# Mixer of a three-part decoder layer: output weight and residual addition on VectorE, behind the multiplication by the inverse deviation, in place of GpSimd

## Chip, cores and metric

The kernel runs on one core of one Trainium2 chip. The time is the device time of one execution in microseconds. PE is TensorE, DVE is VectorE, ACT is ScalarE, POOL is GpSimd and SP is SyncE.

## What is computed

Eight sequences of 256 tokens with 256 features go through three parts, each with a residual addition. The change lies in the second part, the mixer (an mLSTM cell with 4 heads of 64 features), which works on each batch by itself:

```python
x = x + attn(layernorm(x), ...)            # state-space block and gated MLP
x = x + xattn(layernorm(x), ctx, ctx, ...) # the mixer, below
x = x + ffn(layernorm(x), ...)             # FP4-rounded gate, up and down matrices

# mixer, per batch and head
D = exp(log_D - max_log_D)
C = (q @ k.T / sqrt(64)) * D
h = (C / normaliser) @ v
h_norm = (h - mean(h)) / sqrt(var(h) + 1e-5)
h_norm = h_norm * (1.0 + out_w)            # output weight, one number per feature
# transposed back to tokens x features and added to x
```

## The kernel before

The program is written out engine by engine. Semaphores named after events (`hn_ready`, `x2_ready` and so on) tie the engines together, and each engine takes its own instructions strictly in the written order. A batch is two tiles of 128 tokens. `x_res` holds all of x in SBUF as 128 x 16 x 256.

The work has two phases. `front` is the state-space block with its MLP. After it comes `mixer_and_ffn`, in which the mixer (8 batches) and the last part (16 tiles of 128 tokens) run as software pipelines. In each step of a pipeline an engine calls its list of stages, each with a lag: in step s a stage with lag 3 works on batch s - 3. `pipelines` writes the first steps of the mixer out, runs steps 3 to 6 as a hardware loop of two steps in a pass, and then writes out steps in which mixer stages and last-part stages stand in one list (from step 7, five steps). Then comes a loop of the last part alone.

On DVE a mixer step has these stages: `weights` for both chunks (L1541, three multiplications of scores by weights, reading PSUM), `variance` (L1575, sum of squares), `normalise` (the small instructions L1553 to L1560 on the denominators, L1564 twice, the mean L1568, the subtraction L1570) and `scale` (L1580, the multiplication by the inverse deviation `rv`):

```python
mixer = [(lambda b, p: weights(b, p, 0), 1), (lambda b, p: weights(b, p, 1), 1), (variance, 3),
         (normalise, 2), (scale, 3)]
```

ACT computes the exponentials (L1483) and the squares (L1490). POOL has `rstds` (L1635 and L1637, which make `rv` from the sum of squares by a power) and `residual` (L1642, the output weight; L1645, the addition to `x_res`). `normalise` begins with a wait for the additions of earlier batches, because it overwrites the buffer of `h` (two buffers, named `scores` in the profile since they lie in that region) that the addition read:

```python
dve.wait_ge(s["x2_ready"], LEAD + C * (b - 1))
```

In the last part, per tile, DVE takes statistics (L1586, L1591), POOL makes deviation and shift (`tile_rstd`, L1654 to L1660), ACT normalises (L1525), and DVE rounds the tile with the `Quantiser` (L318 to L336; `xq` is its copy for the input, 256 wide, `hq` the one for the hidden rows, 704 wide). PE turns the tile (L1432), multiplies by gate and up (L1443), turns the hidden rows (L1453) and multiplies by down (L1462). DVE adds the result to x (L1618), and SP stores it.

Of the kernel before, what the change touches and what calls it, by code (L numbers as in the profile page):

```python
# [23 lines left out]
ALU = mybir.AluOpType  # L24
# [5 lines left out]
C = S // P  # L30
# [19 lines left out]
LEAD = 8  # L50
# [21 lines left out]
def inner(ap, n):  # L72

    return ap.unsqueeze(len(ap.shape)).to_broadcast([*ap.shape, n])


def middle(ap, n):

    return ap.unsqueeze(1).to_broadcast([ap.shape[0], n, ap.shape[1]])


def carry(eng, m):


    eng.sem_inc(m.carried, 1)
# [51 lines left out]
def pipelines(eng, units, stages, next_units, next_stages, begin, overlap):  # L137


    depth = depth_of(stages) if stages else 0  # L140
    if stages:
        for s in range(depth):
            step(units, stages, s)
        steady(eng, units, stages, depth, min(units, begin))
        for s in range(min(units, begin), begin):
            step(units, stages, s)
    for s in range(overlap):
        step(units, stages, begin + s)
        step(next_units, next_stages, s)
    steady(eng, next_units, next_stages, overlap, next_units)  # L150
    for s in range(next_units, next_units + overlap):
        step(next_units, next_stages, s)
# [1122 lines left out]
def mixer_and_ffn(m):  # L1275
# [14 lines left out]
    h = over_s("h", [P, 2, C * XH, XD])  # L1290
# [4 lines left out]
    s = m.counts["mlstm"]  # L1295
# [29 lines left out]
    @block.sync  # L1325
    def _(sp):
        def load_r(b, p):
            sp.wait_ge(m.max_stored, 16)
            sp.wait_ge(s["arg1_ps"], LEAD + b - 1)
            carry(sp, m)  # L1330
            sp.dma_start(rmax[0:3, p, :].rearrange("j (h t) -> j h t", h=XH),
                         m.rows_dram[bass.ds(b * XH, XH), :, :].rearrange("h j t -> j h t")).then_inc(r_in[p], 16)

        def load_qk(b, p):
            sp.wait_ge(s["qk_ps"], LEAD + C * (b - 1))
            carry(sp, m)
            sp.dma_start(kT[:, p, :, :], m.a["ctxT"][:, :, bass.ds(b * S, S)]).then_inc(arrived[p], 16)
            sp.dma_start(qT[:, p, :, :].rearrange("p k t -> p (k t)"), row(m.xnT, b)).then_inc(arrived[p], 16)

        def load_v(b, p):  # L1340
            sp.wait_ge(s["num_ps"], LEAD + b - 1)
            carry(sp, m)
            for c in range(C):
                sp.dma_start(v[:, p, c, :].rearrange("p (h e) -> p h e", h=XH)[:, :, 0:XD],
                             m.a["ctx"][bass.ds((C * b + c) * P, P), :].rearrange("p (h e) -> p h e", h=XH))\
                  .then_inc(v_in[p], 16)

        sp.wait_ge(t["ones_set"], 1)
        for b in range(2):
            load_qk(b, b)  # L1350
            load_v(b, b)
        for b in range(2):
            load_r(b, b)

        pipeline(sp, B - 2, [(lambda b, p: load_r(b + 2, p), 0), (lambda b, p: load_qk(b + 2, p), 0),
                             (lambda b, p: load_v(b + 2, p), 0)])


        def store(t, p):
            sp.wait_ge(f["y_ready"], LEAD + t + 1)  # L1360
            sp.dma_start(m.out[bass.ds(t, 1), :, :].rearrange("o p d -> (o p) d"), y[:, p, :])\
              .then_inc(y_out[p], 16)

        pipeline(sp, T, [(store, 0)])
        for each in y_out:
            sp.wait_ge(each, LEAD + 16 * (T // 2))
# [166 lines left out]
    def _(dve):  # L1533
        def weights(b, p, c):
            n = C * b + c
            w, done = ((w0, s["w0_exp"]), (w1, s["w1_exp"]))[c]
            dve.wait_ge(s["qk_ps"], LEAD + n + 1)
            dve.wait_ge(done, LEAD + b + 1)
            for k in range(2 if c == 0 else 1):
                mine = (w[:, p, 2 * k:2 * k + 2, :] if c == 0 else w[:, p, :, :]).rearrange("p k t -> p (k t)")  # L1540
                last = dve.scalar_tensor_tensor(mine, bank[3 + k if c == 0 else 5][:], XD ** -0.5, mine, ALU.mult,  # L1541
                                                ALU.mult)
            last.then_inc(s["w_ready"], 1)
# [33 lines left out]
        def scale(b, p):  # L1577
            dve.wait_ge(s["v_rstd"], LEAD + b + 1)
            hp = h[:, p, :, :]
            dve.tensor_tensor(hp, hp, inner(rv[:, p, :], XD), ALU.mult).then_inc(s["hn_ready"], 1)  # L1580


        def tile_stats(t, p):
# [31 lines left out]
        def output(t, p):  # L1615
# [7 lines left out]

        mixer = [(lambda b, p: weights(b, p, 0), 1), (lambda b, p: weights(b, p, 1), 1), (variance, 3),
                 (normalise, 2), (scale, 3)]
        forward = [(product, 3), *first, (tile_stats, 0), (output, 5), (tile_mean, 0), *last]
        pipelines(dve, B, mixer, T, forward, BEGIN, OVERLAP)

    @block.gpsimd
    def _(pool):  # L1630
        def rstds(b, p):
            pool.wait_ge(s["v_ready"], LEAD + b + 1)
            pool.wait_ge(s["hn_ready"], LEAD + b - 1)
            carry(pool, m)
            pool.tensor_scalar(var[:, p, :], var[:, p, :], 1.0 / XD, LN_EPS, ALU.mult, ALU.add).then_inc(s["v_mean"], 1)  # L1635
            pool.wait_ge(s["v_mean"], LEAD + b + 1)
            pool.tensor_tensor(rv[:, p, :], var[:, p, :], m.minus_half[:, 0:C * XH], ALU.pow).then_inc(s["v_rstd"], 1)  # L1637

        def residual(b, p):
            pool.wait_ge(s["hn_ready"], LEAD + b + 1)  # L1640
            rows = h[:, p, :, :].rearrange("p (c h) e -> p c (h e)", c=C)
            pool.tensor_tensor(rows, rows, middle(m.out_w[:], C), ALU.mult).then_inc(s["hn_scaled"], 1)  # L1642
            pool.wait_ge(s["hn_scaled"], LEAD + b + 1)
            here = m.x_res[:, bass.ds(C * b, C), :]
            pool.tensor_tensor(here, here, rows, ALU.add).then_inc(s["x2_ready"], C)  # L1645

        pool.memset(rmax[:], 0.0)
        pool.memset(v[:], 1.0).then_inc(t["ones_set"], 1)


        def tile_rstd(t, p):
            pool.wait_ge(f["f_mv_ready"], LEAD + t + 1)
            carry(pool, m)
            pool.tensor_scalar(ve[:, p, :], mv[:, p, 1:2], LN_EPS, None, ALU.add).then_inc(f["f_ve_ready"], 1)  # L1654
            pool.wait_ge(f["f_ve_ready"], LEAD + t + 1)
            pool.tensor_tensor(rstd[:, p, :], ve[:, p, :], m.minus_half[:, 0:1], ALU.pow).then_inc(f["f_rstd_ready"], 1)
            pool.wait_ge(f["f_rstd_ready"], LEAD + t + 1)
            pool.wait_ge(f["xf_norm"], LEAD + t - 1)
            carry(pool, m)
            pool.tensor_scalar(shift[:, p, :], mv[:, p, 0:1], rstd[:, p, :], -1.0, ALU.mult, ALU.mult)\  # L1660
                .then_inc(f["f_shift_ready"], 1)

        mixer = [(rstds, 3), (residual, 3)]
        forward = [(tile_rstd, 0)]
        pipelines(pool, B, mixer, T, forward, BEGIN, OVERLAP)

# [50 lines left out]
```

## Time and profile before

| | |
|---|---|
| time, median of 3 runs | 661.98 us (651.65, 661.98, 662.48) |
| the profiled execution's own time | 652.93 us |
| its span in the trace | 651.2 us |
| busy: PE, DVE, ACT, POOL | 590.7, 464.6, 242.1, 161.1 us |
| mean granted TensorE clock | 0.953 of full speed |

The span is the time from the first to the last instruction in the trace. Busy times are sums over the whole span; what an engine is worth in one stretch has to be read there. A mean over a group of instructions can hide a few long ones.

### The profile page before, as it was taken

How to read it: one execution, taken by the hardware profiler on the slowest of the kernel's cores; microseconds unless marked ns; L12 is line 12 of the kernel's file. 1: busy time of each engine (PE TensorE's matmuls, PEld its weight loads, DVE VectorE, ACT ScalarE, POOL GpSimd, SP SyncE). 2: the span in 40 equal slices, each digit the busy share in tenths (PEclk: the TensorE clock that was granted, in tenths of full speed). 3: DMA queues.
4: the chain of work that ended last, by engine and by line, in shares of the span. 5: the costliest groups of instructions: out<-in, count | busy, mean ns of one | idle time of the engine just before them, and what ended most of it. 6: DMA issues, size and time to landing. Idle time of an engine off the chain costs nothing. (4 is left out here: it accounts for less than half of the span.)

```text
span 651.2 us, 9629 instructions
## 1 busy us (share of the span) xinstructions
PE 590.7 (91%) x3055; PEld 470.7 (72%) x3055; DVE 464.6 (71%) x983; ACT 242.1 (37%) x532; POOL 161.1 (25%) x199
## 2 busy tenths in 40 slices
PE   5997898699999889899999999869976699999996
PEld 5766465478888778778888888858864466666664
DVE  4999599868886233443444456457898999999994
ACT  1643665744555421211111110154532344444432
POOL 3163003125454101111011010202766322222200
PEclk8997999879999999999999999699985899999999
DMA  9100000000000230000000000134410000000000
GB/s 317 59 1 1 0 2 15 7 5 6 6 4 2 83 147 0 1 1 0 17 17 17 2 17 16 30 90 117 127 49 2 0 10 16 16 16 16 16 17 24
DMA packets 22527, 20.99 MB, mean 32 GB/s; under 512 B 12120, under 2 KB 20696, under 8 KB 22104
## 3 DMA queue, kind: packets, MB, share of 16 engines
q1 hardware_dynamic: 21720, 19.22, 9.2%
q10 hardware_dynamic: 768, 1.26, 0.6%
q8 instruction: 22, 0.36, 0.2%
q14 instruction: 17, 0.14, 0.1%
HBM read 16.04 MB, written 2.34 MB: 28 GB/s over the span
## 5 line engine op out<-in xcount | busy, mean ns | idle before, releaser
L722 PE MATMUL ps<-xnT,w_fc 128*128 128x256 f32 x512 | 112.6, 380 | 0.0
L722 PEld LDWEIGHTS ps<-xnT,w_fc 128*128 128x128 f32 x512 | 96.5, 190 | 12.7
L1443 PE MATMUL ps<-w_fc,scores 128*128 128x352 f32 x256 | 82.9, 478 | 5.9 <-ACT scores L1512 5.9
L1076 DVE TENSOR_TENSOR xs<-ps,xs 128x512 f32<-128x512 f32 x32 | 22.1, 692 | 72.9 <-ACT xs L903 72.9
L1443 PEld LDWEIGHTS ps<-w_fc,scores 128*128 128x128 f32 x256 | 49.1, 197 | 33.3 <-ACT scores L1512 7.4
L903 ACT ACTIVATE xs<-ps 128x512 f32<-128x512 f32 x32 | 19.1, 597 | 107.5 <-PE ps L722 69.9
L735 PE MATMUL ps<-zs,xs 128*128 128x256 f32 x256 | 56.6, 379 | 0.0
L735 PEld LDWEIGHTS ps<-zs,xs 128*128 128x128 f32 x256 | 48.6, 190 | 6.6
L974 DVE SCALAR_TENSOR_TENSOR fold<-xpad,conv_w,fold 128x256 f32<-128x256 f32 x120 | 51.4, 483 | 0.9
L1462 PE MATMUL ps<-u_res,hT 128*128 128x256 f32 x192 | 47.3, 388 | 2.7 <-DVE scores L1618 1.7
L1462 PEld LDWEIGHTS ps<-u_res,hT 128*128 128x128 f32 x192 | 34.9, 189 | 14.8 <-issue 5.3
L624 PE MATMUL ps<-xnT,fold 128*128 128x256 f32 x160 | 39.8, 400 | 2.4 <-ACT xpad L825 2.4
L624 PEld LDWEIGHTS ps<-xnT,fold 128*128 128x128 f32 x160 | 30.2, 199 | 9.8 <-ACT xpad L825 5.8
L561 POOL TENSOR_SCALAR q_ve<-q_mv 128x2 f32<-128x2 f32 x8 | 1.8, 222 | 142.1 <-DVE q_mv L1092 142.1
L543 POOL TENSOR_TENSOR bc<-xs,head_c 128x512 f32<-128x512 f32 x16 | 24.5, 1536 | 49.5 <-DVE zs L1060 29.8
L674 PE MATMUL ps<-xpad,fold 128*128 128x64 f32 x256 | 32.8, 284 | 0.0
L969 DVE TENSOR_SCALAR fold<-xpad,conv_w 128x256 f32<-128x256 f32 x40 | 26.1, 683 | 8.2 <-ACT xpad L825 8.2
L674 PEld LDWEIGHTS ps<-xpad,fold 128*128 128x128 f32 x256 | 31.6, 201 | 0.1
L632 PE MATMUL ps<-fold,xnT 128*128 128x512 f32 x64 | 30.9, 627 | 0.0
L697 PE MATMUL ps<-w_out,xF 128*128 128x256 f32 x128 | 30.2, 380 | 0.3 <-DVE u_res L1067 0.3
L697 PEld LDWEIGHTS ps<-w_out,xF 128*128 128x128 f32 x128 | 23.7, 190 | 6.4 <-issue 3.8
L1483 ACT ACTIVATE xs<-ps,a_tok 128x256 f32<-128x256 f32 (+1 forms) x64 | 20.8, 437 | 18.1 <-PE ps L1379 18.1
(256 smaller groups left out, 1159.0 us busy)
## 6 DMA issues: line engine op xcount, KB each, us to landing
xs<-in_ctxT SPq DMA_DIRECT2D x16, 256.0 KB, 3.3
zs<-in_ffn_w SPq DMA_DIRECT2D x1, 2112.0 KB, 9.4
x_res<-in_x SPq DMA_DIRECT2D x8, 256.0 KB, 7.5
w_fc<-in_w_fc SPq DMA_DIRECT2D x1, 2048.0 KB, 10.4
xs<-xnT SPq DMA_DIRECT2D x8, 256.0 KB, 3.4
xs<-in_ctx SPq DMA_DIRECT2D x16, 128.0 KB, 2.6
out<-scores SPq DMA_DIRECT2D x16, 128.0 KB, 1.7
fold<-in_w_in ACTq DMA_DIRECT2D x2, 580.0 KB, 5.4
```

Of the source, the lines that this page charges most:

```text
L543: pool.tensor_tensor(heads(dx[:, c, :]), heads(m.xs[:, n, :]), inner(m.head_c[:, 2, :], HD), ALU.mult)\
L624: last = pe.matmul(bank[1 + n % 2][:, 0:S], w_in[:, kk, w0:w0 + P], turned_u(b, kk), start=(kk == 0), stop=(kk == KD - 1))
L632: last = pe.matmul(bank[3 + c][:], turned_u(b, kk)[:, c * P:(c + 1) * P], w_in[:, kk, 0:DI], start=(kk == 0), stop=(kk == KD - 1))
L674: last = pe.matmul(bank[2 + c][:, h * HD:(h + 1) * HD], E[:, p, c, h * P:(h + 1) * P], dtx[:, p, c, h * HD:(h + 1) * HD], start=True, stop ...
L697: last = pe.matmul(bank[6][:, c * D:(c + 1) * D], ygT[:, c, k * P:(k + 1) * P], m.w_out[:, k, :], start=(k == 0), stop=(k == DI // P - 1))
L722: last = pe.matmul(bank[half + r][:, i * S:(i + 1) * S], m.w_fc1[:, kk, col:col + P], m.xnT[:, b, kk * S:(kk + 1) * S], start=(kk == 0), s ...
L735: last = pe.matmul(bank[4 + c][:, 0:D], hid[:, p, k, c * P:(c + 1) * P], w_fc2[:, k, :], start=(k == 0), stop=(k == KM - 1))
L969: dve.tensor_scalar(conv[:, p, k, :], xpad[:, p, k, 0:S], m.conv_w[:, ch, 0:1], None, ALU.mult).then_inc(s["conv_step"], 1)
L974: dve.scalar_tensor_tensor(conv[:, p, k, :], xpad[:, p, k, tap:tap + S], m.conv_w[:, ch, tap:tap + 1], conv[:, p, k, :], ALU.mult, ALU.add)\
L1076: dve.tensor_tensor(hid[:, p, 2 * pair:2 * pair + 2, :].rearrange("p k t -> p (k t)"), bank[r][:], gate[:, r, :], ALU.mult).then_inc(g["hi ...
L1443: last = pe.matmul(bank[1 + j][:, 0:HALF], xT[:, p, k * P:(k + 1) * P], m.w_gu[:, k, j * HALF:(j + 1) * HALF], start=(k == 0), stop=(k == ...
L1462: last = pe.matmul(bank[7][:, 0:D], hT[0:w, p, k, :], m.w_dn[0:w, k, :], start=(k == 0), stop=(k == KF - 1))
```

## The change

Of each batch, the two instructions of `residual` move from POOL to DVE and are written right behind `scale`. The semaphores and the values waited for are the same ones. POOL's list of mixer stages keeps `rstds` alone. In the changed kernel the two instructions are L1583 and L1586, and the lines behind them move by 6 on DVE.

```diff
@@ -1578,6 +1578,12 @@
             dve.wait_ge(s["v_rstd"], LEAD + b + 1)
             hp = h[:, p, :, :]
             dve.tensor_tensor(hp, hp, inner(rv[:, p, :], XD), ALU.mult).then_inc(s["hn_ready"], 1)
+            dve.wait_ge(s["hn_ready"], LEAD + b + 1)
+            rows = hp.rearrange("p (c h) e -> p c (h e)", c=C)
+            dve.tensor_tensor(rows, rows, middle(m.out_w[:], C), ALU.mult).then_inc(s["hn_scaled"], 1)
+            dve.wait_ge(s["hn_scaled"], LEAD + b + 1)
+            here = m.x_res[:, bass.ds(C * b, C), :]
+            dve.tensor_tensor(here, here, rows, ALU.add).then_inc(s["x2_ready"], C)
@@ -1635,14 +1641,6 @@
-        def residual(b, p):
-            pool.wait_ge(s["hn_ready"], LEAD + b + 1)
-            rows = h[:, p, :, :].rearrange("p (c h) e -> p c (h e)", c=C)
-            pool.tensor_tensor(rows, rows, middle(m.out_w[:], C), ALU.mult).then_inc(s["hn_scaled"], 1)
-            pool.wait_ge(s["hn_scaled"], LEAD + b + 1)
-            here = m.x_res[:, bass.ds(C * b, C), :]
-            pool.tensor_tensor(here, here, rows, ALU.add).then_inc(s["x2_ready"], C)
@@ -1660,7 +1658,7 @@
-        mixer = [(rstds, 3), (residual, 3)]
+        mixer = [(rstds, 3)]
```

On DVE, at the end of the second step in a pass of the mixer loop, the rows change as follows (`scores` is the buffer of `h`, `rv` the inverse deviation):

```order
@@ -516,4 +519,7 @@
 L1570 SCALAR_TENSOR_TENSOR scores<-h_mean,scores 128x512 [waits post]
 L1580 TENSOR_TENSOR scores<-scores,rv 128x512 [waits v_rstd]
+L1583 TENSOR_TENSOR scores<-scores,out_w 128x512 [waits hn_ready]
+L1586 ISA [waits hn_scaled]
+L1586 TENSOR_TENSOR x_res<-x_res,scores 128x512
 L118 REGISTER_ALU
 L118 COMPARE_AND_BRANCH
```

Two instructions stand behind the scale now, and the second has its wait in an instruction of its own.

On DVE, where mixer and last part stand in one list, the scale of a batch was followed by the quantiser of a tile:

```order
@@ -546,4 +554,6 @@
 L1570 SCALAR_TENSOR_TENSOR scores<-h_mean,scores 128x512 [waits post]
 L1580 TENSOR_TENSOR scores<-scores,rv 128x512 [waits v_rstd]
+L1583 TENSOR_TENSOR scores<-scores,out_w 128x512 [waits hn_ready]
+L1586 TENSOR_TENSOR x_res<-x_res,scores 128x512 [waits hn_scaled]
 L318 TENSOR_REDUCE xq_amax<-scores 128x16 [waits xq_step,xf_norm]
 L320 TENSOR_SCALAR xq_scale<-xq_amax 128x16 [waits xq_step]
```

The two instructions now stand ahead of the quantiser on the same engine.

On POOL, the same place of the program, before:

```order
L1635 TENSOR_SCALAR var<-var 128x8 [waits v_ready,hn_ready]
L1637 TENSOR_TENSOR rv<-var,minus_half 128x8 [waits v_mean]
L1642 TENSOR_TENSOR scores<-scores,out_w 128x512 [waits hn_ready]
L1645 TENSOR_TENSOR x_res<-x_res,scores 128x512 [waits hn_scaled]
L1654 TENSOR_SCALAR f_ve<-f_mv 128x1 [waits f_mv_ready]
L1656 TENSOR_TENSOR f_rstd<-f_ve,minus_half 128x1 [waits f_ve_ready]
```

and in the changed kernel:

```order
L1641 TENSOR_SCALAR var<-var 128x8 [waits v_ready,hn_ready]
L1643 TENSOR_TENSOR rv<-var,minus_half 128x8 [waits v_mean]
L1652 TENSOR_SCALAR f_ve<-f_mv 128x1 [waits f_mv_ready]
L1654 TENSOR_TENSOR f_rstd<-f_ve,minus_half 128x1 [waits f_ve_ready]
L1658 TENSOR_SCALAR f_shift<-f_mv,f_rstd 128x1 [waits f_rstd_ready,xf_norm]
```

Nothing of POOL's queue stands between the inverse deviation of a batch and the small instructions of a tile any more.

## Rows read from the trace of the kernel before

**Rows 1.** Waits, 420 to 515 us: waiter, releaser, total us, times, longest.
```profile
DVE den L1553 <- POOL x_res L1645: 2.0, 4, 0.6
DVE scores L1580 <- POOL rv L1637: 2.4, 1, 2.4
```

**Rows 2.** Chain of waits, one batch of the mixer loop: start us, us, what.
```profile
460.09 0.69 DVE scores L1580
460.85 1.29 POOL scores L1642
462.36 1.27 POOL x_res L1645
```

**Rows 3.** Timeline of DVE, one step of the mixer loop.
```profile
460.69 1.88 DVE L1541 SCALAR_TENSOR_TENSOR xs<-ps,xs 128x512 f32<-128x512 f32 x3
462.49 0.68 DVE L1575 TENSOR_REDUCE var<-scores 128x8 f32<-128x512 f32 x1
463.65 0.17 DVE L1553 TENSOR_SCALAR den<-ps 128x8 f32<-128x8 f32 x1 [0.49 <-POOL x_res L1645]
...
465.40 0.69 DVE L1568 TENSOR_REDUCE h_mean<-scores 128x8 f32<-128x512 f32 x1
466.12 0.69 DVE L1570 SCALAR_TENSOR_TENSOR scores<-h_mean,scores 128x512 f32<-128x512 f32 x1
466.73 0.69 DVE L1580 TENSOR_TENSOR scores<-scores,rv 128x512 f32<-128x512 f32 x1
467.33 1.88 DVE L1541 SCALAR_TENSOR_TENSOR xs<-ps,xs 128x512 f32<-128x512 f32 x3
```

**Rows 4.** Windows of one loop step and of the slow-clock stretch: busy by engine, clock.
```profile
core 0: us, PE busy (x) PEld busy (x) DVE busy (x) ACT busy (x) POOL busy (x), PEclk, DMA share, GB/s
...
466.70:473.30 6.60, 5.79 (x47) 4.98 (x47) 5.81 (x14) 3.23 (x9) 4.38 (x4) 1.00 0.56 153
...
486.80:496.20 9.40, 4.56 (x21) 3.97 (x20) 8.84 (x20) 1.64 (x3) 5.58 (x7) 0.50 0.01 3
```

**Rows 5.** Chain of waits where PE takes over, and one gate group later.
```profile
515.10 1.50 PE ps L1453 x6
516.60 5.80 PE ps L1443 x16
...
526.20 4.90 PE ps L1443 x16
```

**Rows 6.** Instructions of line L1558, register part: times in ns, min/median/max.
```profile
L1558 DVEq FUSED_REGOPS  x4: 57/64/64, 450.8 to 470.7; - x4
```

**Rows 7.** Timeline of DVE in the written-out steps.
```profile
483.04 0.68 DVE L1575 TENSOR_REDUCE var<-scores 128x8 f32<-128x512 f32 x1
483.63 0.16 DVE L1553 TENSOR_SCALAR den<-ps 128x8 f32<-128x8 f32 x1
...
485.97 0.69 DVE L1570 SCALAR_TENSOR_TENSOR scores<-h_mean,scores 128x512 f32<-128x512 f32 x1
486.79 0.69 DVE L1580 TENSOR_TENSOR scores<-scores,rv 128x512 f32<-128x512 f32 x1
```

**Rows 8.** Timeline of DVE and POOL beside the quantiser.
```profile
487.56 1.26 POOL L1642 TENSOR_TENSOR scores<-scores,out_w 128x512 f32<-128x512 f32 x1 [0.80 <-DVE scores L1580]
487.85 1.01 DVE L320 TENSOR_SCALAR xq_scale<-xq_amax 128x16 f32<-128x16 f32 x1
...
488.98 1.26 POOL L1645 TENSOR_TENSOR x_res<-x_res,scores 128x512 f32<-128x512 f32 x1
489.18 1.34 DVE L324 SCALAR_TENSOR_TENSOR xq_v<-xq_inv,scores 128x256 f32<-128x256 f32 x1
...
507.69 0.96 DVE L320 TENSOR_SCALAR xq_scale<-xq_amax 128x16 f32<-128x16 f32 x1
...
509.13 0.36 DVE L324 SCALAR_TENSOR_TENSOR xq_v<-xq_inv,scores 128x256 f32<-128x256 f32 x1
```

**Rows 9.** Lines L320 and L324, input quantiser: ns min/median/max, first and last start.
```profile
L320 DVE TENSOR_SCALAR xq_scale<-xq_amax x16: 156/165/1008, 487.9 to 620.4; 128x16 f32<-128x16 f32 x16
L324 DVE SCALAR_TENSOR_TENSOR xq_v<-xq_inv,scores x16: 360/361/1341, 489.2 to 621.1; 128x256 f32<-128x256 f32 x16
```

## Prediction

> **The bound.** I read first where the two moved operations lie in the program, then who waits for whom there, then the order of DVE's own instructions, because the work moves onto DVE. The span is 651.2 us and the profiled execution took 652.93, so 1.73 us lie outside it. The moved operations run only between 453.5 and 508.6 us. In the view of waits for the mixer [rows 1] DVE waits four times, 2.0 us in all, for POOL's residual addition, and once, 2.4 us, for POOL's inverse deviation. The chain of waits [rows 2] confirms the first one: scale on DVE (460.09), output weight on POOL (460.85), addition on POOL (462.36), and 3.56 us after the scale began, DVE's `normalise` of a later batch (463.65). A reader of the chain alone would say that POOL bounds this loop.
>
> The timeline of DVE says something else [rows 3]. One step of the loop is 6.64 us, from the L1541 group at 460.69 to that at 467.33. DVE works through all of it except the 0.49 us ahead of L1553. The POOL part of the chain lies beside work that DVE has to do anyway: three multiplications of weights (L1541, 1.80 us until the next start) and the variance sum (L1575). So DVE's own queue and the loop through POOL are nearly equal, and DVE is the one that has almost nothing left to give. PE is busy 5.79 of 6.60 us in a step at full clock [rows 4], but it waits for nobody's output on the chain there. After 515.10 us the chain is PE's all the way to 634 us (each tile has one gate and up group, as at 526.20, [rows 5]). A delay of DVE before 515.10 is therefore passed on whole to the end, and nothing after it hides or enlarges it.
>
> **Added work.** The output weight and the addition do not run on DVE in this trace, but `scale` itself (L1580, 0.69 us) is a TENSOR_TENSOR of the same size and type with both inputs in SBUF. I take its duration. What counts on the queue is the distance between starts. Where the next instruction needs the result of the one before, it is 0.72 us: L1568 at 465.40, L1570 at 466.12 [rows 3]. Where it does not, it is 0.60: L1580 at 466.73, L1541 at 467.33. Before, `scale` took 0.60 of the queue. After, scale to weight is 0.72, weight to addition 0.72, addition to the next group 0.60, together 2.04. The cost is 2.04 - 0.60 = 1.44 us per batch, and for 8 batches 11.5 us. The bounds are 8 x 1.20 = 9.6 (no dependent gap) and 8 x 1.6 = 12.8 (a further 0.16 each). In the loop, which runs for the first four batches, the addition gets its place in `x_res` from a register, and the order shows a separate instruction for the wait in front of it. The nearest thing is L1558, which takes its place from a register too: four times, once for each pass through a loop step, DVE's sequencer spends 0.06 us on it [rows 6]. With the separate wait I take 0.1 us x 4 = 0.4, with bounds 0 and 0.5.
>
> **Removed time.** (1) The wait at L1553 for the addition. By starts, L1575 to L1553 is 463.65 - 462.49 = 1.16 us in the loop, and 0.59 where nothing waits (483.04 to 483.63, [rows 7]). The difference is 0.57; the four places have 0.56, 0.57, 0.56 and 0.66, together 2.35 us (the 2.0 of [rows 1] is without the overlap of starts). After the change the addition is earlier in DVE's own queue, so this wait is gone entirely. Next late there would be PE's sums, but PE works 5.8 us per step [rows 4] against DVE's new 7.6. Or scale would wait for POOL's inverse deviation: POOL's two small instructions are 4.38 - 1.28 - 1.27 = 1.83 us [rows 2, 4], behind the 0.68 of L1575 and with some 0.4 for the handing over, so 2.9 us after L1575 begins; DVE asks 466.73 - 462.49 - 0.57 = 3.67 after it. That is late by nothing. (2) A short wait of scale for POOL's inverse deviation for batch 5, where POOL came late because of its two long instructions: 0.82 us from L1570 at 485.97 to L1580 at 486.79 [rows 7] in place of 0.61 (466.12 to 466.73), so 0.2 us. The later wait of 2.4 us [rows 1] stays: POOL runs the tile's three small instructions ahead of batch 7's deviation, and both start from DVE results whose distance does not change. DVE keeps its idle 2.4 us there, in front of the added work and not behind it, so it hides none of it.
>
> (3) The largest and least visible term. In three places the quantiser's small instructions take far longer than elsewhere [rows 8]: L320 1.01 us at 487.85 and 0.96 at 507.69, L324 1.34 us at 489.18, though their medians over 16 are 0.165 and 0.361 [rows 9]. Each time they end with an instruction of POOL: POOL's output weight runs from 487.56 to 488.82 and L320 ends at 488.86; POOL's addition runs from 488.98 to 490.24 and L324 ends at 490.52, that is 0.28 us later. At 509.13 POOL is idle, and the same L324 takes 0.36. The next batch repeats the pattern (L320 1.01, L324 1.34). So while POOL runs one of its two long two-input instructions, these DVE instructions stand still. With the change POOL has none left. The gain is 2 x (0.84 + 0.98) + 0.79 = 4.4 us, bounds 0 and 4.4. The DVE instructions beside POOL in the loop (L1541, which reads PSUM, and the one-input L1575) have their usual 0.68 us each, so nothing is to be gained there.
>
> The Trainium skill ("Advanced Engine Details and Errata", section VectorE Performance Modes) says that the second SBUF port of VectorE is shared with GPSIMD and that the two block each other. This trace agrees, by the ends of the rows just named. The same rule speaks against the change too ("GPSIMD Engine Reference", Key points: contention also with two-input VectorE instructions): both new ones have two SBUF inputs and could hold up POOL's deviation. If each held it for a whole instruction behind which DVE then waited, that would be up to 8 x 0.7 us more. Here POOL is idle while they run, since its next input comes from DVE's next variance or statistics, and the sum stays.
>
> **The sum.** +11.5 +0.4 -2.35 -0.2 -4.4 = +5.0 us on the profiled 652.93, so 657.9. The three runs shown are 651.65, 661.98 and 662.48: the profiled execution is one of the short kind, and what makes the other kind 10 us longer is not in this trace. The change touches none of it that I can see, so I set the same +5.0 against the median: 661.98 + 5.0 = 667.0 us, 0.8% more. Two places can move it by a little. The bounds of the terms give +2.7 to +6.4 with the stalls gone. And when PE begins the long stretch at 515.10, its first gate and up group ran partly at the lower clock, 5.80 us in place of the 4.90 of a later tile [rows 5]; whether that 0.9 us comes again depends on when the clock falls.
>
> **Rivals.** First, the stalls of L320 and L324 stay, because they belong to the quantiser's first tiles or to POOL's small instructions. Then 4.4 us are not given back: +9.4, 671.4 us. The ends that coincide in four places speak against it. Second, the change gains, as the chain of waits suggests: if the weights and the variance sum found another place, the 3.56 us from scale to normalise would become 2.04, four times 1.5 us, against 4 x 1.44 for the other batches, and with the stalls and the short wait gone the sum is -6.1 + 5.8 - 4.6 = -4.9, 657.1 us. DVE takes its queue in order and has 0.5 us free in a step, which speaks against it. Third, on the other side: PE's clock. The loop step grows from 6.6 to about 7.6 us while PE's work stays near 6.0, so PE would be idle about 1.5 us in each. It stood at 1.00 through the loop, and at 0.50 in the stretch where PE worked 4.56 of 9.40 us [rows 4]. If the idle time were enough to let it fall to 1.2 GHz in the loop, PE's step would double and PE would set the step in place of DVE. It decides as soon as PE's step is over 7.6 us. Twice 5.8 and the handing over is 12, and at 4.4 us more for four steps that is +17.6 on top, 684.6 us, slower by 3.4%. Against it: the stretch from 466.7 to 473.3 has 0.8 us of idle time and stays at full clock, and 1.5 in 7.6 is nearer to that (12% and 20% idle) than to the 51% of the stretch at 0.50. That the residual is not really moved can be excluded: the order shows it gone from POOL.
>
> **The numbers.** The forecast, +3 to +7 us, 0.76. Stalls stay 0.10. The gain of the chain 0.04. PE's clock 0.08. Something unseen 0.02. A measurement of this kernel can tell about 2% from no change. The forecast, the stalls and the chain's gain all lie within it: with half of the unseen 0.91; slower by over 2% is the clock case, 0.08; faster 0.01. The range runs from 655 to 672: the top holds the forecast's bounds and the case of the stalls on the median, the bottom holds the chain's gain (657.1) and the forecast on the short kind of run (656 to 660). It leaves out the clock and the unseen, 0.10.
>
> **To look for.** Two DVE groups of 8 at 0.69 us each; no instruction of POOL over 1 us in the mixer but the deviation of 1.65; no wait of L1553 for anyone in the loop; the loop's step at 7.5 to 7.6 us; L320 and L324 at their medians in all 16 tiles; PE idle 1 to 1.5 us per step and its clock still 1.00 until about 487; the 2.4 us wait for the deviation of batch 7 still there; PE's long stretch beginning near 520 in place of 515.10 and as long as before. I am wrong if the two additions are longer than 0.8 us, if L320 is still 1 us, or if the clock drops inside the loop.

## Result and profile after

The changed kernel took 659.86 us, median of 4 runs (657.97 to 668.24), beside 656.82 for the kernel before (651.29 to 662.48, 4 runs). The ratio is 1.012, 95% interval 1.007 to 1.017. In a second measurement with more runs it was 1.012 again, interval 1.009 to 1.015: slower by 1.2%, small but clear of no change. The profiled execution took 657.97 us against 652.93, the +5.0 of the forecast; over the runs the 1.2% are nearly 8 us. Both kernels have runs some 10 us longer, which the ratios leave out; with them the medians lie nearer together than the ratio says.

The timeline of DVE for one step of the mixer loop, to be laid beside [rows 3]:

```profile
459.88 0.69 DVE L1580 TENSOR_TENSOR scores<-scores,rv 128x512 f32<-128x512 f32 x1
460.60 0.69 DVE L1583 TENSOR_TENSOR scores<-scores,out_w 128x512 f32<-128x512 f32 x1
461.44 0.69 DVE L1586 TENSOR_TENSOR x_res<-x_res,scores 128x512 f32 x1
462.05 1.88 DVE L1541 SCALAR_TENSOR_TENSOR xs<-ps,xs 128x512 f32<-128x512 f32 x3
463.85 0.67 DVE L1575 TENSOR_REDUCE var<-scores 128x8 f32<-128x512 f32 x1
464.44 0.15 DVE L1553 TENSOR_SCALAR den<-ps 128x8 f32<-128x8 f32 x1
...
469.66 1.88 DVE L1541 SCALAR_TENSOR_TENSOR xs<-ps,xs 128x512 f32<-128x512 f32 x3
```

Both new instructions take 0.69 us. From L1580 to the next group is 2.17 us in place of 0.60. L1553 starts 0.59 us behind L1575 and waits for nobody. The step is 7.61 us (462.05 to 469.66) in place of 6.64.

Where mixer and last part mix, the quantiser's instructions that were at 1.01 and 1.34 us [rows 8] are short. First the timeline of DVE at the first of these places, then the views of the two lines (ns, min/median/max) that answer [rows 9]:

```profile
492.29 0.69 DVE L1586 TENSOR_TENSOR x_res<-x_res,scores 128x512 f32<-128x512 f32 x1
492.90 0.41 DVE L318 TENSOR_REDUCE xq_amax<-scores 128x16 f32<-128x256 f32 x1
493.35 0.17 DVE L320 TENSOR_SCALAR xq_scale<-xq_amax 128x16 f32<-128x16 f32 x1
...
493.84 0.42 DVE L324 SCALAR_TENSOR_TENSOR xq_v<-xq_inv,scores 128x256 f32<-128x256 f32 x1
```

```profile
L320 DVE TENSOR_SCALAR xq_scale<-xq_amax x16: 157/164/175, 493.3 to 624.7; 128x16 f32<-128x16 f32 x16
L324 DVE SCALAR_TENSOR_TENSOR xq_v<-xq_inv,scores x16: 360/361/425, 493.8 to 625.4; 128x256 f32<-128x256 f32 x16
```

The maxima have fallen from 1008 and 1341 ns to 175 and 425. The windows of three loop steps show what PE does meanwhile (the columns are those of [rows 4], PEclk third from the end):

```profile
462.00:469.60 7.60, 6.01 (x50) 5.17 (x48) 7.11 (x16) 3.23 (x9) 1.83 (x2) 1.00 0.38 106
469.60:477.30 7.70, 6.20 (x37) 5.54 (x35) 7.20 (x17) 3.23 (x9) 1.83 (x2) 0.75 0.37 103
477.30:485.40 8.10, 8.10 (x40) 6.47 (x41) 7.60 (x18) 3.12 (x9) 1.83 (x2) 0.60 0.15 33
```

PE idles 1.5 us in a step, ahead of its score group. In the group behind the second of these pauses (it starts at 471.69) its clock falls to 1.2 GHz, and it is back at 2.4 GHz within some 10 us. DVE's steps keep their length meanwhile (the next one begins at 477.28, 7.62 us on). The clock has a price later. The timeline of PE has the second gate and up group at 7.94 us, which was 4.97 before, and DVE waits for it ahead of its second product:

```profile
511.89 7.94 PE L1443 MATMUL ps<-w_fc,scores 128*128 128x352 f32 x16 [3.93 <-issue]
```

```profile
520.66 0.89 DVE L1602 TENSOR_TENSOR hf<-ps,sg 128x704 f32<-128x704 f32 x1 [1.24 <-ACT sg L1506]
```

The chain of waits behind it:

```profile
511.89 7.96 PE ps L1443 x16
...
520.53 0.59 ACT scores L1525
521.12 0.28 ACT scores L1512
521.40 0.26 issue
521.66 4.97 PE ps L1443 x16
```

ACT turns to the next tile only behind the silu (`sg`, L1506) that the product needs, so the third group starts at 521.66. It runs at full clock; before it was the group of 5.80 us [rows 5]. The place of the low clock has moved by one group.

**The whole account**, by starts, from the mixer's second group of weights (441.06 before, 439.86 after): to the first product of the last part 64.71 and 71.05 us, from there to the last output addition (L1618, now L1624: 648.47 and 652.70) 142.70 and 141.79. So the mixer lost 6.34, and the rest, with the third stall of L320 gone and the clock moved, gave back 0.91: +5.43. Ahead of this stretch the changed kernel's trace was 1.20 us earlier, and after the start of the last output addition it ended 0.77 later: +5.0.

### The profile page after: what moved, and what is told of

Same layout as the page of the kernel before. It is cut to its first block and busy times, and to the rows that moved or that the text cites. A ratio compares the mean times of both kernels' runs of the same rounds, so it can differ in the third digit from the quotient of the medians.

```text
span 656.2 us, 9629 instructions
## 1 busy us (share of the span) xinstructions
PE 594.5 (91%) x3055; PEld 474.1 (72%) x3055; DVE 469.3 (72%) x999; ACT 242.6 (37%) x532; POOL 141.3 (22%) x183
```

## Experiments

Where an experiment is read in its trace I use the same stretch, from the mixer's second group of weights to the last output addition: 207.41 us before, 212.84 changed. Two kernels were traced twice: the changed one gave 212.84 and 214.15, the split one of experiment 7 gave 204.66 and 203.25. A difference of up to 1.4 us between two traces is therefore not an effect by itself; most of it arises behind the first product. Experiments 2, 3, 4, 5 and 8 and the changed kernel of experiment 10 were executed once (661.12, 666.47, 662.86, 667.41, 653.14 and 667.53 us); they have no ratio and are read from their trace alone.

**1. The wait alone.** POOL keeps the residual; DVE's wait moves down behind the denominators, to the instruction that needs it (L1564).

```diff
 def normalise(b, p):
-    dve.wait_ge(s["x2_ready"], LEAD + C * (b - 1))
...
+    dve.wait_ge(s["x2_ready"], LEAD + C * (b - 1))
     for c in range(C):
...
```

> The kernel before, with POOL's residual as it was, but DVE's wait for the addition moved inside normalise from its first instruction to the one that overwrites h (L1564), behind the four small instructions on the denominators. If the wait at L1553 was the 0.57 us per step that the starts show, the small instructions (0.8 us) cover it: the loop step falls from 6.64 to 6.07 us, 2.3 us in all, ratio 0.996. Rival: POOL's handing over is the real bound, then the wait only shows again at L1564 and the step stays at 6.6.

Ratio 0.996, interval 0.994 to 0.998. The timeline of DVE, one step:

```profile
469.12 1.88 DVE L1541 SCALAR_TENSOR_TENSOR xs<-ps,xs 128x512 f32<-128x512 f32 x3
...
475.27 1.88 DVE L1541 SCALAR_TENSOR_TENSOR xs<-ps,xs 128x512 f32<-128x512 f32 x3
```

The step is 6.15 us, not 6.07: 0.08 more per step than expected. It lies ahead of L1564, which starts 0.34 us behind the reciprocal in place of 0.24 (472.21 to 472.55 here, 464.37 to 464.61 in the trace before); the wait in front of it is what is new there. The stretch is 205.15 us, -2.3. So the handing over to POOL was not the bound; all that the long chain through POOL cost in the loop was this half microsecond of badly placed waiting.

**2 to 4. What stops the quantiser.** To the changed kernel come two idle POOL instructions of 128x512 per batch on a buffer of their own; nobody waits for them. The second differs in place, the third in kind.

```diff
-        mixer = [(rstds, 3)]
+        mixer = [(rstds, 3), (twin, 3)]
+        def twin(b, p):
+            pool.wait_ge(s["x2_ready"], LEAD + C * (b + 1))
...
+            pool.tensor_tensor(w, w, w, ALU.mult).then_inc(s["twin"], 1)
...
+            pool.tensor_tensor(w, w, w, ALU.mult).then_inc(s["twin"], 1)
```

The second waits for `hn_ready` of its batch (DVE's scale) in place of `x2_ready`:

```diff
-            pool.wait_ge(s["x2_ready"], LEAD + C * (b + 1))
+            pool.wait_ge(s["hn_ready"], LEAD + b + 1)
```

The third has one input in both instructions, and a semaphore increment for which nobody on the other engines waits ahead of each:

```diff
-            pool.tensor_tensor(w, w, w, ALU.mult).then_inc(s["twin"], 1)
+            pool.tensor_scalar(w, w, 1.0, None, ALU.mult).then_inc(s["twin"], 1)
```

> The changed kernel, plus two idle two-input multiplications of 128x512 on POOL per batch on a buffer of its own, behind the addition. Nothing waits for them. If POOL's two-input work is what stops the quantiser, L320 and L324 are again at about 1.0 and 1.3 us where they follow the mixer's addition (3 and 2 times of 16), and the mixer is some 4 us longer than in the changed kernel. Rival: the quantiser's first tiles are slow for another reason or were slow because of waiting; then they stay at 0.17 and 0.36-0.42 us.

> As the run before, but the two idle POOL multiplications start behind the multiplication by the inverse deviation, so beside DVE's output weight and addition, which have two inputs in SBUF too. If two-input instructions of DVE stand still beside them, L1583 or L1586 take about 1.3 us in place of 0.69, 4 to 8 us in all. If only some forms are stopped, they stay at 0.69 and only the quantiser's L320 right behind them is late.

> As the run with the twins behind the addition, but the idle POOL instructions read one tensor (TENSOR_SCALAR, 128x512). If it is POOL's holding of a port for the whole instruction, L320 and L324 are late here too, by what is left of POOL's instruction at their start. If only POOL's two-input form stops DVE, they stay at 0.17 and 0.36-0.42 us.

Two inputs, behind the addition; the timeline of POOL (the buffer `spare` is the idle work's), then that of DVE:

```profile
493.65 1.04 POOL L1650 TENSOR_TENSOR spare<-spare 128x512 f32<-128x512 f32 x1 [2.68 <-DVE x_res L1587]
494.77 1.04 POOL L1653 TENSOR_TENSOR spare<-spare 128x512 f32<-128x512 f32 x1
```

```profile
493.94 0.79 DVE L320 TENSOR_SCALAR xq_scale<-xq_amax 128x16 f32<-128x16 f32 x1
...
495.05 1.04 DVE L324 SCALAR_TENSOR_TENSOR xq_v<-xq_inv,scores 128x256 f32<-128x256 f32 x1
```

L320 ends at 494.73, 0.04 behind the end of POOL's first instruction, L324 at 496.09, 0.28 behind the second: the same distances as in [rows 8]. It is the same for the next batch (0.78 and 1.05 us); for the last one only the end of POOL's work meets L320, which takes 0.43. So it is POOL's two-input work that stops them, and not what it computes or who waits. POOL's instructions were 1.04 us here (one tensor is both inputs) and 1.27 before, so the stretch grows by 2.4 us over the changed kernel and not by 4.

Two inputs, beside DVE's own pair (L1584 and L1587 are its weight and addition here); POOL, then DVE:

```profile
463.50 1.45 POOL L1650 TENSOR_TENSOR spare<-spare 128x512 f32<-128x512 f32 x1 [1.66 <-DVE scores L1581]
465.03 1.37 POOL L1653 TENSOR_TENSOR spare<-spare 128x512 f32<-128x512 f32 x1
```

```profile
463.36 0.69 DVE L1584 TENSOR_TENSOR scores<-scores,out_w 128x512 f32<-128x512 f32 x1
464.20 1.30 DVE L1587 TENSOR_TENSOR x_res<-x_res,scores 128x512 f32 x1
465.42 0.68 DVE L1542 SCALAR_TENSOR_TENSOR xs<-ps,xs 128x512 f32<-128x512 f32 x1
```

It goes both ways. POOL starts under DVE's L1584 and takes 1.45 us, 0.41 more than alone; DVE's L1587 starts at 464.20, while that one has 0.75 us to go, and takes 1.30 in place of 0.69. POOL's second starts under L1587, which has 0.47 to go, and takes 1.37 in place of 1.04. So in each of the three overlaps the later instruction is longer by nearly all that the earlier one had left: 0.41 of 0.55, 0.61 of 0.75, 0.33 of 0.47. The weights (L1542), with one input in PSUM, run beside POOL's second instruction and keep their 0.68. The stretch is 218.80 us, +6.0, within the 4 to 8 expected. Had the change left such work on POOL at this place, it would have cost about twice as much. This is the effect that the Trainium skill ("GPSIMD Engine Reference", Key points) names for two-input instructions, with a size here.

One input, behind the addition; POOL, then DVE:

```profile
497.04 1.51 POOL L1651 TENSOR_SCALAR spare<-spare 128x512 f32<-128x512 f32 x1 [2.47 <-DVE x_res L1587]
```

```profile
497.18 0.50 DVE L320 TENSOR_SCALAR xq_scale<-xq_amax 128x16 f32<-128x16 f32 x1
```

L320 takes 0.50 us and ends at 497.68, long before POOL's instruction does; L324 behind it takes 0.43, no more than in the changed kernel. Here and at two more places (506.83 to 507.46, 517.88 to 518.53) a one-input instruction of POOL stopped L320 for about its first 0.6 us, not for its length. Neither of the two outcomes expected; it lies between. The stretch was still 2.6 us longer than in the changed kernel, the larger part for another reason: these two held POOL 3.2 us, and its deviation came late for DVE's scale, by 0.17, 0.88 and, for the last batch, 0.50 us (2.69 in place of 2.19).

**5. The same work, one step later.** On DVE, the pair leaves `scale` and becomes a stage of its own, `residual`, a step later.

```diff
-        mixer = [(lambda b, p: weights(b, p, 0), 1), (lambda b, p: weights(b, p, 1), 1), (variance, 3),
+        mixer = [(lambda b, p: weights(b, p, 0), 1), (lambda b, p: weights(b, p, 1), 1), (variance, 3), (residual, 4),
```

> The changed kernel, with DVE's output weight and addition of a batch one step later, between the variance sum and normalise. The first one no longer follows its producer directly (0.1 us less per batch), and batch 6's pair lies in the 2.2 us in which DVE waits for POOL's last deviation. If that wait can be filled, the mixer is 2.4 us shorter than in the changed kernel. Rival: the pair has two inputs in SBUF and now runs beside POOL's variance and power instructions, which it holds up; then the deviation comes up to 0.7 us later and the gain is 1 to 1.7 us.

The rival's mechanism held. The timeline of POOL shows its deviation for batch 7 at 2.18 us in place of 1.65, behind a variance instruction of 0.44 in place of 0.20, beside DVE's pair (514.98 and 515.77):

```profile
515.27 0.44 POOL L1644 TENSOR_SCALAR var<-var 128x8 f32<-128x8 f32 x1 [0.35 <-DVE var L1575]
515.80 2.18 POOL L1646 TENSOR_TENSOR rv<-var,minus_half 128x8 f32<-128x8 f32 x1
```

DVE's wait for it was still 1.55 us in place of 2.19. To the first product it was 69.77 us, 1.28 less than in the changed kernel, as the rival had it, and there DVE waited 0.90 us for a first gate group of 7.5 us at the lower clock. Behind the first product nothing of the gain was left: the stretch was 213.10, with a later group partly at that clock (6.43 us).

**6. The clock.** Transposes of the identity fill PE's pauses, results unused: six in each step of the mixer, more around the first gate groups.

```diff
-        mixer = [(scores1_even, 1), (scores0, 1), (scores1_odd, 1), (sums, 2), (args, 0)]
-        forward = [(turn_x, 2), (turn_h, 4), (gate_up, 2), (down, 4)]
+        def filler(k, times):
+            for _ in range(times):
+                pe.transpose(bank[k][:, 0:P], m.ident[:], m.ident[:])
...
+        mixer = [(scores1_even, 1), (scores0, 1), (scores1_odd, 1), (fill_mixer, 1), (sums, 2), (args, 0)]
+        forward = [(fill_turn, 2), (turn_x, 2), (turn_h, 4), (fill_gate, 2), (gate_up, 2), (down, 4)]
```

> The changed kernel, with transposes of the identity on PE (results unused) in the idle stretches of PE in the mixer and at the start of the last part, so that the clock stays up. If the clock costs time, the second gate group falls from 7.9 to 4.9 us, DVE's wait of 1.2 us for it goes, and PE's long stretch starts 1.5 us earlier: 656 to 657 us. If DVE alone sets the pace until 519.4 us and PE's lower clock lies beside it, the time is that of the changed kernel, 658 us; if the transposes get in PE's way, more.

Ratio to before 1.019, interval 1.010 to 1.028, where 656 to 658 us (1.005 to 1.008) were expected. That is not the price of the transposes: in the trace (668.02 us) the mixer's first group of weights starts at 445.76, 9.56 us later than in the changed kernel's, and no transpose stands ahead of it. The stretch is the better measure. The clock stayed at 1.00 through the loop, yet DVE's step stayed 7.61 us: the fall of the clock there costs nothing. The changed kernel of experiment 10, which has no transposes in the mixer, confirms it: in its trace the clock did not fall in the loop, with the same pauses of 1.5 us in front of it, and it took 71.02 us to the first product, against 71.05 where the clock fell. The second gate group was 4.97 us, and from the first product to the last output 140.46 us passed in place of 141.79, a gain of 1.3. In the mixer's first two steps, where PE is the bound, the fillers cost 1.2. The stretch was 212.71, so what they gave and what they cost cancel.

**7. Only the two batches that pay.** The late wait, and weight and addition on DVE for batches 5 and 6, on POOL for the others; in `scale`:

```diff
+            if isinstance(b, int) and b in ON_DVE:
+                dve.wait_ge(s["hn_ready"], LEAD + b + 1)
...
+                dve.tensor_tensor(rows, rows, middle(m.out_w[:], C), ALU.mult).then_inc(s["hn_scaled"], 1)
...
+                dve.tensor_tensor(here, here, rows, ALU.add).then_inc(s["x2_ready"], C)
```

> The kernel before with the wait for the addition ahead of L1564, and with output weight and addition on DVE for batches 5 and 6 alone, whose POOL instructions stopped L320 and L324; POOL keeps the other six. By the measured terms: -2.3 for the wait, and for the two batches -2 x 1.8 for the stalls and -0.2 for POOL's late deviation against +2 x 1.53 on DVE. That makes -3.1 us, ratio 0.995. Rival: the terms do not add, because PE's clock or the wait for the last deviation takes it back; then it is that of the run with the late wait, 0.996, or above.

> The split kernel once more, unchanged, beside the others on the same chip. The trace of the first run had the mixer and the rest 2.75 us shorter than before, which the times did not show (0.999, interval 0.994 to 1.004). If the times only scattered over the clock's levels ahead of the mixer, this one is near 0.996; if the split itself costs something outside the part that I compared, it is again at 0.999 or above.

The stretch was 204.66 us, -2.75, and the one stall left (L320 at 0.96 us for batch 7) is as it should be. The times did not follow: 0.999 (0.994 to 1.004), and in the second measurement 0.999 again (0.996 to 1.002). The trace of the second (655.13 us) shows where they went. Its stretch is 203.25 us, shorter still, although its first gate group ran wholly at the lower clock (7.81 us at 501.19) and held up the first product by 0.5. But the mixer's second group of weights starts at 447.28 in it, and at 441.16 in the first trace of the same kernel (650.40 us): 6.1 us are lost ahead of everything that the edit touches. Such losses go with the granted clock. The runs at 0.952 took 647.69 to 649.08 us, some 3 us less than the kernel before at 0.953; those at 0.945 took about 655. So the stretch is shorter by 2.75 and 4.16 us, and a gain of the whole execution is not shown; why this kernel's executions so often lose time ahead of the mixer stays open.

**8. Half of the change.** Output weight on DVE, addition on POOL. Against the changed kernel:

```diff
-            dve.tensor_tensor(here, here, rows, ALU.add).then_inc(s["x2_ready"], C)
...
+            pool.wait_ge(s["hn_scaled"], LEAD + b + 1)
...
+            pool.tensor_tensor(here, here, rows, ALU.add).then_inc(s["x2_ready"], C)
```

> Half of the change: output weight on DVE, addition on POOL. DVE has 0.72 us more per batch, POOL's addition ends ahead of normalise, so the wait at L1553 is gone and the loop step is 6.8 us (before 6.64, changed 7.6). Of the stalls only L320's is left (POOL has one long instruction in place of two), three times about 0.8 us. Together some +1.2 us against before in the mixer. Rival: if the wait is about handing over to POOL and not about its length, L1553 still waits and the step is 7.3.

The loop step was 6.79 us, as expected, and the stretch 208.55, +1.1, near the +1.2 expected but no more than two traces of one kernel differ by. To the first product it was 66.35 us, +1.64. L320 took 1.08 us twice, and at the third place, where a stall was expected too, 0.16.

**9 and 10. Fillers at two places.** Ahead of the second gate group and of the first turning of hidden rows, in the split kernel (10 and 13 of them) and in the changed one (20 and 10), whose edit this is:

```diff
+        def fill_turn(t, p):
+            if isinstance(t, int) and t == 2:
+                filler(10)
...
+        def fill_gate(t, p):
+            if isinstance(t, int) and t == 1:
+                filler(20)
```

> The split kernel (late wait, batches 5 and 6 on DVE), plus transposes of the identity on PE (results unused) at two places only: ahead of the second gate group and ahead of the first turning of hidden rows, where PE stood idle 2 to 3 us before a group at the lower clock. If the clock there costs the 0.9 us of the group and 0.8 us of the turn, the stretch from PE's first hidden turn to the last output is 1 to 1.7 us shorter than the split kernel's 133.3. Rival: the transposes are too few or late to hold the clock, or delay the turn; then it is 133.3 or more.

> The changed kernel with the same transposes at those two places (20 and 10), none in the mixer. In the changed kernel the second gate group took 7.9 us at the lower clock and DVE waited 1.2 us for it. If that is the clock's price, the second group takes 4.9 us, DVE's wait goes and PE's long stretch begins 1 to 1.5 us earlier after the first product, without the 1.2 us that the fillers cost in the mixer's first steps.

In both, second and third gate groups took 4.97 us. With the changed kernel, the third began 9.41 us after the first product in place of 10.75. Both lost the gain again at the end, where the last tiles leave PE with pauses: from the first product to the last output addition it was 142.90 us (split kernel without fillers 142.63) and 141.78 (changed 141.79). The timeline of PE in the split kernel with fillers:

```profile
634.48 3.02 PE L1463 MATMUL ps<-u_res,hT 128*128 128x256 f32 x12 [1.69 <-DVE scores L1640]
...
639.62 4.74 PE L1463 MATMUL ps<-u_res,hT 128*128 128x256 f32 x12 [1.00 <-ACT hT L1515]
```

One of the last groups of the down multiplication runs at the lower clock, 4.7 us in place of 3.05. Which one, or none, differs from trace to trace. Measured over runs, the split kernel with fillers has the lowest ratio of all: 0.994, interval 0.992 to 0.996, median 648.54 us. That interval meets the one of experiment 1 (0.994 to 0.998), so that it beats the late wait alone is not shown. Of the price that I expected, the trace confirms the groups, and not the stretch, which was 133.57 us from the first hidden turn, where 133.3 or more was the rival's sign.

**11. The changed kernel again.**

> The changed kernel once more, unchanged, for its ratio with more runs. By the terms read in its trace, +5.4 us from the mixer's second batch to the last output: ratio 1.008. The first measurement gave 1.012 with an interval from 1.007 to 1.017, with +1 us of it unexplained by those terms; if that is a level of the clock ahead of the mixer, this one falls to 1.008; if it is a cost of the change, it stays at 1.012.

1.012, interval 1.009 to 1.015, so not a chance of the first measurement. Its trace has the stretch at 214.15 us, 1.31 more than the first one, and that is again one late down group: 4.61 us at 645.63. The end of the span came 3.86 us after the start of the last output addition; in the kernel before it was 2.73. That is regular: 3.5 to 4.0 us in all seven traces with the pair directly behind scale on DVE for every batch, 2.7 to 2.8 in the seven others. The rows there, one output addition and its DMA, are the same. The profile's view of transfers has 18 or 19 of kind instruction in queue q14 in these seven and 17 in six of the others; but experiment 5 has 18 and the short end, so these alone do not explain it. By the traces the 1.2% are then, as an estimate, 0.8 for the stretch (DVE's queue), 0.1 to 0.2 for this end, whose cause is open, and up to 0.2 for a clock that falls in the last tiles, as it did in one of the two traces.

## The prediction, step by step

**The bound was read rightly.** DVE's queue set the loop's pace on both sides. The predicted 7.6 us per step was 7.61.

**The price of the pair was 0.4 us too small.** The 0.69 and the 0.72 behind scale are right. From weight to addition it is 0.80 us in the written-out steps and 0.84 in the loop, where I had 0.72 and 0.82. That makes 4 x 1.56 + 4 x 1.52 = 12.3 us in place of 11.9. The row that I used for the dependent distance (L1568 to L1570) has a small second tensor, and the addition has two of 128x512; that this makes the 0.08 is a guess that no run tests.

**The wait went entirely**, 2.35 us, as experiment 1 and the step's 0.59 show; the short one for batch 5 went too, and the one of 2.4 us stayed at 2.2.

**The stalls went, and were worth 4.0 us rather than 4.4.** Measured from scale to the next variance sum, less the pair, the two double stalls gave 1.48 and 1.75 us in place of 1.82 each (L324 is 0.42 and not 0.36 where it follows directly, and at the first place DVE stands 0.20 ahead of the tile's statistics), the single one 0.76. The rival that they would stay is refuted by the rows above, and its reason by experiment 2, in which POOL's two-input work alone brings them back.

**The rival of PE's clock happened and did not have its price.** I gave it 0.08 and expected that a fall of the clock in the loop makes PE the bound. The clock fell, for about one step. PE's 9.6 us for that step (471.69 to 481.28, from one score group to the next) used up the lead that it had over DVE and no more. That it would stay at 1.00 until 487 was wrong. So was the point that I named, PE's step over 7.6 us: in the step of 9.6 us DVE did not wait. By my own sign, a clock that drops inside the loop, I should have been wrong; the sign was badly chosen. Whether the clock falls there is also not settled by the step: of four traces with the step of 7.61 us and pauses of 1.5 it fell in two (the changed kernel's) and held in two (experiment 2 and the changed kernel of experiment 10).

**The rival of the chain** (a gain of 4.9 us) failed as argued; experiment 1 shows that its true content was a wait at the wrong instruction.

**The median.** The change of +5.0 on the profiled execution was right to 0.1 us, partly by luck. Up to the first product the mixer lost 6.34 us where my terms give 5.7; behind it 0.91 came back where I had 0.8. That is +5.4, and of what lay outside the stretch, which I had not considered, 1.20 less ahead of it and 0.77 more behind it happened to bring it to 5.0. The second trace of the changed kernel is at +7.75, and over the runs the change costs 1.2%, nearly 8 us, more than the +3 to +7 of the forecast: the forecast left out the end of the span and the late falls of the clock, and had the pair and the stalls wrong by 0.4 each. The 667.0 was set on 661.98 us for the kernel before, whose median over the four runs of the result was 656.82; the changed kernel's was 659.86.

## To carry along

When the chain of waits alternates between two engines, read the queue of each: work moved onto the engine that has only half a microsecond free per step costs its length less that half (here 1.56 us less 0.6), whatever the chain loses. Try first to move the wait to the instruction that needs it; here that cost nothing and gained 0.4%, the opposite sign of the change. Where an instruction's maximum is several times its median (here 1008 ns and 165), lay its end beside the ends of other engines' instructions; here that named the cause.

## Not expected of the hardware

- DVE and POOL exclude each other both ways when each has a long instruction with two inputs in SBUF: DVE's 0.69 us became 1.30, POOL's 1.04 became 1.45. DVE's tiny TENSOR_SCALAR on SBUF (L320) is stopped as well (0.17 us became 1.01); the weights with an input in PSUM (0.68 us) are not.
- A one-input instruction of POOL of 1.5 us stopped DVE's L320 only for about its first 0.6 us, at three places of one trace.
- TensorE's clock fell from 2.4 to 1.2 GHz in a loop in which PE was busy 6.0 of 7.6 us in two traces, and stayed up in two others with the same step and the same pauses; it also stayed up at 5.8 of 6.6 and with fillers. Where it fell, the loop's step was the same 7.61 us.
